# First expert layer: last layer feature-major with 512 moving columns, gates broadcast through memory, one turn back at the end

## The reference

```python
def _swiglu_stacked(x, w1, b1, w2, b2, w3, b3):
    p1 = jnp.einsum('btd,ndh->nbth', x, w1) + b1[:, None, None, :]
    p2 = jnp.einsum('btd,ndh->nbth', x, w2) + b2[:, None, None, :]
    glu = jax.nn.silu(p1) * p2
    return jnp.einsum('nbth,nhd->nbtd', glu, w3) + b3[:, None, None, :]
scores = jax.nn.softmax(x @ gate_w + gate_b, axis=-1)
weights, indices = jax.lax.top_k(scores, K)          # K = 2
routed = sum of weights * routed_all at indices
shared = _swiglu_stacked(x, sw1, sb1, sw2, sb2, sw3, sb3).mean(axis=0)
return shared + routed
```

## Time and profile before

| | us |
|---|---|
| median of 3 runs | 569.26 |
| lowest, highest | 567.64, 570.02 |
| the profiled execution | 567.78 |
| its span, first to last instruction | 566.0 |
| TensorE busy in it | 414.9 (73%) |
| VectorE busy in it | 411.7 (73%) |
| ScalarE busy in it | 244.2 (43%) |
| GpSimd busy in it | 109.6 (19%) |

### The profile page before, as it was taken

How to read it: one execution, slowest core, us unless ns; L and a number is a source line. 1 busy time by engine, 2 the same in 40 slices (tenths; PEclk the granted TensorE clock), 3 DMA queues, 4 the chain that set the end, 5 groups by cost and what they waited for, 6 DMA issues and landing times.

```text
span 566.0 us, 8533 instructions
## 1 busy us (share of the span) xinstructions
PE 414.9 (73%) x3355; PEld 271.8 (48%) x3358; DVE 411.7 (73%) x867; ACT 244.2 (43%) x419; POOL 109.6 (19%) x63
## 2 busy tenths in 40 slices
PE   4997799999995773648979663799981578748115
PEld 2465376566664351314645443667761145533005
DVE  4797456475449868499778884857897899875974
ACT  3756532222223132458987531443531233333941
POOL 2100000079200000396000000200098143300000
PEclk9799799999997576768988795899995657777757
DMA  7940000000004300000000000300000000000001
GB/s 265 356 128 3 0 1 2 0 1 0 1 1 162 137 2 1 1 0 1 1 1 2 1 0 1 57 0 1 1 0 1 2 0 2 1 2 0 0 0 38
DMA packets 11068, 16.60 MB, mean 29 GB/s; under 512 B 5258, under 2 KB 9748, under 8 KB 10132
## 3 DMA queue, kind: packets, MB, share of 16 engines
q1 hardware_dynamic: 10740, 15.26, 7.9%
q10 hardware_dynamic: 288, 0.79, 0.4%
HBM read 15.52 MB, written 0.52 MB: 28 GB/s over the span
## 4 chain that ended last, share of the span: by engine, by line
PE 52%; DVE 33%; ACT 9%; issue 5%; DMA 1%; ACTq 0%; DVEq 0%
PE ps L818 6%; PE ps L823 6%; PE ps L833 6%; PE ps L1675 4%; PE ps L1684 4%; ACT arena L1468 4%; PE ps L1840 2%; PE ps L1411 2%; PE ps L1397 2%; PE ps L514 2%; PE ps L1383 2%; DVE l2buf L1761 2%; DVE arena L615 2%; PE ps L298 2%; PE ps L528 2%
## 5 line engine op out<-in xcount | busy, mean ns | idle before, releaser
L904 DVE SCALAR_TENSOR_TENSOR arena<-ps,cols,arena 128x512 f32<-128x512 f32 x40 | 29.8, 750 | 48.6 <-PE ps L823 46.6
L869 ACT ACTIVATE arena<-ps,cols 128x512 f32<-128x512 f32 x40 | 27.5, 687 | 69.5 <-PE ps L818 69.5
L1468 ACT ACTIVATE arena<-ps,const 128x512 f32<-128x512 f32 x80 | 48.8, 707 | 4.4 <-PE ps L1383 4.0
L1527 DVE TENSOR_SCALAR arena<-arena 128x512 f32<-128x512 f32 x80 | 41.8, 551 | 11.8 <-ACT arena L1468 10.5
L833 PEld LDWEIGHTS ps<-weights,arena 128*128 128x128 f32 x320 | 38.6, 192 | 8.6 <-issue 8.5
L833 PE MATMUL ps<-weights,arena 128*128 128x128 f32 x320 | 39.2, 276 | 0.2 <-DVE x_tm L893 0.2
L818 PE MATMUL ps<-h_fm,weights 128*128 128x512 f32 x80 | 38.6, 606 | 0.0
L823 PE MATMUL ps<-h_fm,weights 128*128 128x512 f32 x80 | 37.6, 592 | 0.0
L1769 POOL TENSOR_TENSOR l2buf<-l2buf,arena 128x1024 f32<-128x1024 f32 x8 | 25.4, 3215 | 47.1 <-DVE l2buf L1761 47.1
L1383 PE MATMUL ps<-l2buf,picks_b 128*128 128x256 bf16 x160 | 28.3, 307 | 7.7 <-ACT arena L1468 4.6
L573 ACT ACTIVATE arena<-arena 128x1024 f32<-128x1024 f32 x16 | 16.9, 1057 | 34.2 <-POOL arena L594 26.8
(11 more groups left out here) (311 smaller groups left out, 875.4 us busy)
## 6 DMA issues: line engine op xcount, KB each, us to landing
weights<-in_moe_w SPq DMA_DIRECT2D x2, 2048.0 KB, 10.1
weights<-in_moe_w SPq DMA_DIRECT2D x3, 1280.0 KB
l2buf<-in_picks SPq DMA_DIRECT2D x1, 1664.0 KB, 9.7
rows<-in_rows SPq DMA_DIRECT2D x1, 1216.0 KB, 13.9
x_tm<-in_x SPq DMA_DIRECT2D x2, 256.0 KB, 5.2
ctx_fm<-in_ctx_fm ACTq DMA_DIRECT2D x1, 512.0 KB, 6.0
ctx_tm<-in_ctx SPq DMA_DIRECT2D x1, 512.0 KB, 15.2
mats<-in_mats SPq DMA_DIRECT2D x1, 512.0 KB, 14.9
```

Source lines behind the costliest of these rows:

```text
L1468: AC.activation(hats[:, u % 2, 2 * c:2 * c + 2, :].rearrange("p r c -> p (r c)"), ps[:, m % 3, :], ACT.Abs, bias=const[:, C_NEGM:C_NEGM + ...
L1527: V.tensor_scalar(v, v, 1.0, -1.0, ALU.min, ALU.add).then_inc(hat_ok, 1)
```

## The change

The last layer is computed feature-major: w3's block is stationary and 512 tokens of `glu` move, two matmuls per unit instead of eight. Its result has features on partitions and tokens along the row, so the gate is now a row and no longer one number per partition. SyncE writes the transposed gates (10 x 1024) to memory and reads each routed expert's row of 1024 back onto all 128 partitions, into one of four buffers. The units are summed in a new feature-major tile `total`: shared ones with the factor 1/2, routed ones as a product (`weighed`) and a sum. After the last unit, for each half, TensorE turns `total` back with eight matmuls (four of them the biases, which before stood in the middle), VectorE adds the result to x_tm and takes the statistics. ScalarE's copy of the gates moves ahead of unit 5's silus. Eleven loads now share one (`rest_in`), and whoever needs one of them waits for all; the load of `wq8` moves up to the others. Below, the same replacement of semaphores at L401, L586, L984 and L1163 is left out.

```diff
@@ -169,9 +169,9 @@
             G.wait_ge(pool_chain, chained["pool"])
 
 
-        x_in, const_in, ctxf_in, ctxt_in = [sem("x_in0"), sem("x_in1")], sem("const_in"), sem("ctxf_in"), sem("ctxt_in")
-        rows_in, cols_in, mats_in = sem("rows_in"), sem("cols_in"), sem("mats_in")
-        rows0_in = sem("rows0_in")
+        x_in, const_in, ctxf_in, rest_in = [sem("x_in0"), sem("x_in1")], sem("const_in"), sem("ctxf_in"), sem("rest_in")
+        cols_in, rows0_in = sem("cols_in"), sem("rows0_in")
...
@@ -365,7 +365,7 @@
                 ins.then_inc(kx_ready, 1)
...
+                dve.wait_ge(rest_in, REST)
                 dve.wait_ge(v_ps, g + 1)
                 V.tensor_tensor(vdup[:, g], ps[:, banks[g % nb], :].rearrange("p (b e) -> p b e", b=4),
...
@@ -752,9 +752,8 @@
             s = lambda name: sem(f"moe0_{name}")
             lg_ps, gates_ok, gT_ps, gT_ok = s("logits"), s("gates"), s("gatesT"), s("gatesT_sb")
             shifted, powered = s("less_max"), s("exp")
-            by_ps = s("bias_ps")
             up_ps, silu_ok, glu_ok, y_ps, y_added = s("up_ps"), s("silu"), s("glu"), s("y_ps"), s("y_added")
-            lin_ps = s("lin_ps")
+            lin_ps, spread_in, x_ps = s("lin_ps"), s("gates_spread"), s("x_ps")
             lg = arena[:, 0:64].rearrange("p (j e) -> p j e", j=NT)
             pr = arena[:, 64:128].rearrange("p (j e) -> p j e", j=NT)
             t1 = arena[:, 128:192].rearrange("p (j e) -> p j e", j=NT)
@@ -766,6 +765,10 @@
             gT = arena[0:NQ, 512:512 + T]
             silu = arena[:, 2048:2048 + 1024].rearrange("p (k t) -> p k t", k=2)
             glu = arena[:, 4096:4096 + 2048].rearrange("p (i k t) -> p i k t", i=2, k=2)
+            gates_dram = nc.dram_tensor("gates_T", (NQ, T), F32, kind="Internal").ap()
+            weighed = arena[:, 1536:2048]
+            total = arena[:, 3072:4096].rearrange("p (h t) -> p h t", h=2)
+            gate_rows = [arena[:, 6144 + T * i:6144 + T * i + T] for i in range(4)]
             units = [(e, half) for e in (*range(NE, NQ), *range(NE)) for half in range(2)]
             SHARED = 2 * NSH
 
@@ -825,14 +828,23 @@
 
                 def down(u):
                     e, half = units[u]
-                    pe.wait_ge(glu_ok, 2 * u + 2)
                     if u >= 2:
                         pe.wait_ge(y_added, u - 1)
-                    for t in range(4):
-                        for k in range(2):
-                            ins = PE.matmul(ps[:, 4 + u % 2, P * t:P * t + P], glu[:, u % 2, k, P * t:P * t + P],
-                                            w3[:, e, k, :], start=(k == 0), stop=(k == 1))
+                    for k in range(2):
+                        pe.wait_ge(glu_ok, 2 * u + k + 1)
+                        ins = PE.matmul(ps[:, 4 + u % 2, :], w3[:, e, k, :], glu[:, u % 2, k, :],
+                                        start=(k == 0), stop=(k == 1))
                     ins.then_inc(y_ps, 1)
+
+                def turn_back(half):
+
+                    pe.wait_ge(y_added, len(units) - 1 + half)
+                    for j in range(4 * half, 4 * half + 4):
+                        PE.matmul(ps[:, 6 + half, P * (j % 4):P * (j % 4) + P], gT[:, j * P:j * P + P], b3[:],
+                                  start=True, stop=False)
+                        ins = PE.matmul(ps[:, 6 + half, P * (j % 4):P * (j % 4) + P],
+                                        total[:, half, P * (j % 4):P * (j % 4) + P], ident, start=False, stop=True)
+                    ins.then_inc(x_ps, 1)
 
                 pe.wait_ge(moe0_in, 96)
                 up(0)
@@ -851,13 +863,20 @@
                             for j in range(4):
                                 ins = PE.transpose(ps[0:NQ, 6 + k, P * j:P * j + P], gates[:, 4 * k + j, :], ident)
                             ins.then_inc(gT_ps, 1)
-                        pe.wait_ge(gT_ok, 2)
-                        for k in range(2):
-                            for j in range(4):
-                                ins = PE.matmul(ps[:, 6 + k, P * j:P * j + P],
-                                                gT[:, (4 * k + j) * P:(4 * k + j + 1) * P], b3[:], start=True, stop=True)
-                            ins.then_inc(by_ps, 1)
                     down(u)
+                turn_back(0)
+                turn_back(1)
+
+            @block.sync
+            def _(sp):
+                sp.wait_ge(gT_ok, 2)
+                sp.dma_start(gates_dram, gT[:]).then_inc(spread_in, 16)
+                sp.wait_ge(spread_in, 16)
+                for e in range(NE):
+                    if e >= 4:
+                        sp.wait_ge(y_added, SHARED + 2 * (e - 4) + 2)
+                    sp.dma_start(gate_rows[e % 4], gates_dram[e].partition_broadcast(P)).then_inc(spread_in, 16)
+                    sp.wait_ge(spread_in, 16 * e + 32)
 
             @block.scalar
             def _(act):
@@ -870,7 +889,7 @@
                     if u == 1:
                         act.wait_ge(shifted, 1)
                         AC.activation(pr, t1, ACT.Exp).then_inc(powered, 1)
-                    if u == SHARED + 1:
+                    if u == SHARED:
                         for k in range(2):
                             act.wait_ge(gT_ps, k + 1)
                             AC.activation(gT[:, 512 * k:512 * k + 512], ps[0:NQ, 6 + k, :], ACT.Copy).then_inc(gT_ok, 1)
@@ -883,17 +902,19 @@
 
                 def accumulate(u):
                     e, half = units[u]
-                    if u == SHARED:
-                        dve.wait_ge(gates_ok, 1)
                     dve.wait_ge(y_ps, u + 1)
-                    if u >= 2:
+                    y = ps[:, 4 + u % 2, :]
+                    if u < 2:
+                        V.tensor_scalar(total[:, half], y, 1.0 / NSH, None, ALU.mult).then_inc(y_added, 1)
+                    elif u < SHARED:
                         dve.wait_ge(y_added, u - 1)
-                    for t in range(4):
-                        j = 4 * half + t
-                        ins = V.scalar_tensor_tensor(out=x_tm[:, j], in0=ps[:, 4 + u % 2, P * t:P * t + P],
-                                                     scalar=gates[:, j, e:e + 1], in1=x_tm[:, j],
-                                                     op0=ALU.mult, op1=ALU.add)
-                    ins.then_inc(y_added, 1)
+                        V.scalar_tensor_tensor(out=total[:, half], in0=y, scalar=1.0 / NSH, in1=total[:, half],
+                                               op0=ALU.mult, op1=ALU.add).then_inc(y_added, 1)
+                    else:
+                        dve.wait_ge(spread_in, 16 * e + 32)
+                        dve.wait_ge(y_added, u)
+                        dve_link(V.tensor_tensor(weighed, y, gate_rows[e % 4][:, 512 * half:512 * half + 512], ALU.mult))
+                        V.tensor_tensor(total[:, half], total[:, half], weighed, ALU.add).then_inc(y_added, 1)
 
                 for u, (e, half) in enumerate(units):
                     for k in range(2):
@@ -909,29 +930,24 @@
                         probabilities(dve)
                     if u == 3:
                         second(dve)
-                    if u == SHARED + 1:
-                        dve.wait_ge(y_added, SHARED - 1)
-                        for k in range(2):
-                            dve.wait_ge(by_ps, k + 1)
-                            dve_link(V.tensor_tensor(x_tm[:, 4 * k:4 * k + 4], x_tm[:, 4 * k:4 * k + 4],
-                                                     ps[:, 6 + k, :].rearrange("p (j d) -> p j d", j=4), ALU.add))
                     if u >= 2:
                         accumulate(u - 2)
                     if u == 8:
                         input_scales(dve)
                 accumulate(len(units) - 2)
-                dve.wait_ge(y_added, len(units) - 1)
-                all_stats(range(4))
                 accumulate(len(units) - 1)
-                dve.wait_ge(y_added, len(units))
-                all_stats(range(4, NT))
+                for half in range(2):
+                    x4 = x_tm[:, 4 * half:4 * half + 4]
+                    dve.wait_ge(x_ps, half + 1)
+                    dve_link(V.tensor_tensor(x4, x4, ps[:, 6 + half, :].rearrange("p (j d) -> p j d", j=4), ALU.add))
+                    all_stats(range(4 * half, 4 * half + 4))
                 V.sem_inc(x_done, 1)
 
 
         wn = sb("wn", [P, 9, P])
         wT = sb("wT", [P, 9, P])
         halves_done = sem("halves_done")
-        ffn3_in, scales_ok, wq_ok, wT_ps, wT_ok = (sem("ffn3_in"), sem("scales"), sem("ffn3_w"), sem("ffn3_wT_ps"),
+        scales_ok, wq_ok, wT_ps, wT_ok = (sem("scales"), sem("ffn3_w"), sem("ffn3_wT_ps"),
                                                     sem("ffn3_wT"))
         blocks = wn[:].rearrange("p c (g i) -> p (c g) i", i=32)
...
@@ -939,16 +955,16 @@
         @block.sync
         def _(sp):
             for i, name in enumerate(("w_gate", "w_up")):
```

(48 more changed lines are left out.)

## The result

The changed kernel took 572.96 us in the median of 7 runs (570.69 to 577.58), the kernel before 569.12 (567.44 to 570.60): ratio 1.0077, 95% interval 1.0040 to 1.0114. It is slower by 3.8 us; forecast were 569.5, no change, and a range to 573.0. The profiled execution took 573.43 us (span 571.6) against 567.78 (566.0).

The account below looks back on a forecast made before the run. TensorE's own stream was taken to bound the expert stage. Terms -1.1 - 2.9 + 0.1 + 1.7 + 3.3 = +1.1 us on 567.8 gave 568.9 profiled; forecast median 569.5, range 566.5 to 573.

Parts of the forecast that it names:

- The last layer: Each unit's last layer on TensorE: 4 records, 1.72 us against 1.78; -1.1 us over nineteen units.
- The 40% by the Trainium skill: Rival at the last layer: it falls to 40% of its time, 20 units save 21 us, total 548; chance 0.03.
- The middle: TensorE from gate transposes to unit 6's input layers: 2.70 us instead of 5.61, saving 2.9.
- The gates through memory: Gates' write and first read before unit 4's accumulation: landing at 102.8, VectorE waits 2 us, TensorE not; +0.1 us.
- The addition against GpSimd: VectorE's accumulation additions wait for running GpSimd instructions, stopping TensorE 1.3 us near 120.5; +1.7 us with a second stop.
- The second possible stop (0.4): Unit 8's addition, asked for at 124.05, costs 0.75 us if GpSimd's cast is first, else nothing; put at 0.4.
- The end: Turning back after the last unit: about 1.9 us a half, next stage at 180.35 instead of 177.05; +3.3 us.
- The bound of 4.5 us: Upper bound of the cost of turning back after the last unit, if the clock falls before the work is out.
- the forecast's +3.1 at the end: From the last unit's last layer to the next stage: 7.35 us (173.0 to 180.35) against 4.29 before.
- what the prediction had to leave open: GpSimd's two memsets of 3.5 us: by the rule they cost VectorE's additions nothing, but no run showed it.

Follow-up runs that it names:

- padded: Changed kernel with the bias products' operands filled with zeros from 10 to 128 rows, alternation with identity products kept: 569.33 us, 0.9994 of the kernel before.
- repaired versions: Six variants of the changed kernel that compute everything, with turn backs reordered, padded or relieved of the bias calls, some with accumulation drawn ahead: medians 568.29 to 569.98 us.
- ten-row run: Changed kernel with each identity call of the turn backs replaced by a second bias call, leaving out the experts' sum: 569.13 us in one run.
- both alternating ones: The changed kernel itself, 572.96 us, and its variant with bias operands zero-padded to 32 rows, 573.73 us in one run.
- grouped: Changed kernel with the four bias calls of each half put before its four identity calls: 568.74 us, 0.9992 of the kernel before.
- run ahead from 9: Version zero-padded to 128 rows, with accumulate(u-2) in front of unit u's products from unit 9 on: 569.05 us, 1.0002 of the kernel before.

## Why the prediction was wrong

- The last layer: right. 5.15 us a unit from 5.22, 0.07 gained against 0.06. The 40% by the Trainium skill (TensorE: Matmul & The Clock Gate, Back-to-back issue gap) didn't happen; records stand 0.43 apart (79.66 to 81.37 for four).
- The middle: right. 95.11 to 97.70 is 2.59 us, saving 3.0 against 2.9. ScalarE's later silus stopped nobody.
- The gates through memory: right in effect. From the copy (96.83) to the first use (102.61) 5.8 us where 7.4 was reckoned; VectorE waited 0.5, TensorE not at all.
- The addition against GpSimd: right in place (unit 9, L976's 4.11 us, one stop), too dear: 2.19 us instead of 0.69, but it ended 0.2 after GpSimd and not 0.69, so the stop was 0.5 and not 1.3. The second possible stop (0.4) didn't come: the forecast left open which would be first, and the addition started at 124.15, GpSimd's cast at 124.16. Together 1.2 too much.
- The end: wrong, and this decides. The step that failed reads "The bias records stood 0.123 apart, the plain ones 0.111, so about 1.9 a half". The 0.123 was no spacing: the 1.97 us from 95.47 to 97.44 in the earlier trace rows are 16 records at 0.111 and one change of height at 0.19. So before's trace held the cost of a change, spread over 16 records, and the forecast took the mean over to a place where the height changes at every call. A half measured 3.33 and 5.65. The bound of 4.5 us ("the clock falls before the work is out") was named but is too small for what came; the end was +8.5. With padded operands the same end took 7.4 us, and the sum had 7.35: the arithmetic was sound for operands of one height.
- Sum: -3.4 until the last unit and the forecast's +3.1 at the end would have been level, as the repaired versions are. With +8.5 it is +5.1 in the profile and +3.8 in the medians.

## What to carry to other kernels

Price a matmul by its neighbours, not by its own shape: where the row count of the stationary operand changes between calls, 0.19 us came on top here, the length of a weight load, so group calls of one height or pad the short ones with zeros. A burst of short-row matmuls can lower the granted clock while TensorE is fully busy, and the rest of the burst pays (2.3 us here; the stages behind were not longer, 387.76 against 388.95). Moving work from a full stream to a serial end is worth only what its price there is; and draw a VectorE addition of two SBUF tiles clear of GpSimd's long instructions before putting anything urgent behind it.

## What the runs showed of the hardware

- A change between 10 (or 32) and 128 rows of the stationary operand costs 0.19 us; none of it with 128 on both sides (0.112 a record) or 10 on both (0.112). The Trainium skill (TensorE: Matmul & The Clock Gate, The mechanism) says that weight loads overlap with running matmuls only where the row group differs; the same section also has them drawn ahead into a background buffer. Here loads of the same 128 rows started beside the running matmuls, and the ones behind a change of height did not.
- The clock fell from 1.00 to 0.50 with TensorE busy 1.00 of 1.00 us, in the ten-row run and in both alternating ones, and held to the end of the work in the padded and grouped ones. What share of rows, at what spacing, it takes was not tried.
- A VectorE addition with two SBUF inputs waits for a running GpSimd instruction that reads SBUF and ends 0.2 to 0.55 us after it (2.19 and 3.50 us instead of 0.69; 2.19 and 2.24 in the two later cases of the run ahead from 9). The wait goes the other way too: where the addition started first, by 0.01 us, GpSimd's cast took 3.49 us (changed kernel, the last two lines of the fence) instead of 2.96 (before, the line behind it).
- Beside GpSimd's memsets the additions took their plain 0.69 (first pair below, changed kernel). With this the Trainium skill's rule (SBUF — State Buffer, Who interferes with whom), that one which only writes doesn't contend, agrees; it settles what the prediction had to leave open.

```profile
127.60 3.51 POOL L1009 MEMSET kexp<- 128x4096 f32 x1
...
129.09 0.69 DVE L917 TENSOR_TENSOR arena<-arena 128x512 f32<-128x512 f32 x1
...
124.15 0.69 DVE L917 TENSOR_TENSOR arena<-arena 128x512 f32<-128x512 f32 x1
124.16 3.49 POOL L1007 CAST picks_b<-l2buf 128x3328 bf16<-128x3328 f32 x1
```

```profile
125.65 2.96 POOL L988 CAST picks_b<-l2buf 128x3328 bf16<-128x3328 f32 x1
```
